# Layer 0 of a two-layer graph network in loops: the column that neighbouring windows share moves to TensorE, the kernels' products go by array halves behind the tiles

## The chip, the cores and the metric

The kernel runs on one NeuronCore of a Trainium2 chip. Five engines work side by side, each with an instruction queue of its own: TensorE (PE, its weight loads shown as PEld), VectorE (DVE), ScalarE (ACT), GpSimd (POOL) and SyncE (SP). They meet by semaphores alone. The metric is the device time of one execution in microseconds, lower is better. "Issue" in a profile is time in which an engine waited for nothing that the profile shows; "ACTq" is what ACT's queue itself runs, such as register instructions.

## The reference

There are 3125 nodes with 64 channels and 53125 edges, sorted by their target `dst`. Layer 0 is a spline convolution: an edge's three attributes give eight weights, its message is the sum over eight kernels of weight times `x[src] @ W[k]`, messages are averaged over the edges of a target, `x @ root` is added, then batch norm and ELU. Layer 1 sums `x[src] + edge_attr_64` over the edges of a target and applies a two-layer perceptron with batch norm. Each layer is added to its input and normalised.

```python
xj = x[src]
z = (B[:, :, None] * xj[:, None, :]).reshape(Etot, S * x.shape[1])
msg = z @ W.reshape(S * x.shape[1], W.shape[2])
agg = jax.ops.segment_sum(msg, dst, num_segments=x.shape[0])
cnt = jax.ops.segment_sum(jnp.ones((Etot,), dtype=x.dtype), dst, num_segments=x.shape[0])
out = agg / jnp.maximum(cnt, 1.0)[:, None] + x @ root
# layer 1
agg = jax.ops.segment_sum(node_feats[src] + edge_feats, dst, num_segments=n_nodes)
h = jax.nn.relu(agg @ W1 + b1) @ W2 + b2
```

## The kernel before

Edges are cut into T = 416 **tiles** of 128, one edge a partition, and eight tiles are a **chunk** (CH = 8, NCH = 52 chunks). As targets are sorted, a tile's targets lie in a **window** of WIN = 12 nodes from `base[g]` on. The next tile's window may begin with the target at which this one ends, so the two share a column.

*Per chunk.* POOL gathers `x[src]` for the chunk four ahead into `rows[:, s, t, 0:64]` with eight indirect DMAs (L296), once the z products of the slot's last chunk are done (`z_done`, L293). SP loads 256 KB of `edge_attr_64` into the other half of `rows` at the same moment (L249). Their loops are hardware loops over four chunks; PE, ACT and DVE have their 52 chunks written out.

DVE builds from comparisons with an iota, for the chunk ahead: `hot` (L730, position in the window), `whot` (L735, hot times eight weights and a one, fp32), `pair` (L746, source block and window position, bf16) and `ohp` (L752, source within its block, bf16).

*Per tile* (L404 to L417). PE runs `count_pairs(g + 1)` (L373), the counts of edges between 125 sources and 25 x 12 (block, window position) pairs, into one of MB = 3 banks of PSUM; the z product (L412), `rows` times `whot`, two fp32 passes; and `add_shared(g + 1)` (L380). For that, ACT's `keep_pairs(g)` copies the 25 counts of the column that the next window begins with into `shared` (L544), and PE adds them to the next tile's bank by an identity matrix.
*At the close of a chunk* PE counts edges (`count_edges`, L393, two fp32 passes over `ones`), sums the z of edge attributes (L385) and runs the eight 64 x 64 kernels (L388, two fp32 passes each) on `z_sb`, ACT's copy of z (L554, two halves), all into `t_ps`. DVE adds the eight windows of `t_ps` into `agg` two chunks later (L763), in order, each waiting for the one before. `whot` is built again only when `t_ready` says that the kernels are done (L733).

*After the loop* PE turns `agg` to node-major by 25 transposes of 65 partitions (L449, count included), DVE divides by the count, adds `xroot` and goes on with batch norm. Layer 1 multiplies a three-part bf16 table by `adj` (L473 over the whole array, L481 by halves of the array in turn).

Of the kernel before, what the change touches and what calls it, by code (L numbers as in the profile page):

```python
# [6 lines left out]
I32 = mybir.dt.int32  # L7
U8 = mybir.dt.uint8
F8 = mybir.dt.float8e4
BF16 = mybir.dt.bfloat16  # L10
# [5 lines left out]
def gnn_two_layers(nc, x, src, dst, ea3, ea64, wk_d, root_d, gamma0, beta0,  # L16
# [11 lines left out]
    AHEAD = SLOTS  # L28
    GATHERED = CH * 16
# [9 lines left out]
    NB = -(-NT // TPB)  # L39
    FULL = E // P  # L40
# [6 lines left out]
    MB = 3  # L47
# [14 lines left out]
    with ctx:  # L62
# [8 lines left out]
        idx = sb("idx", [P, SLOTS, CH], I32)  # L71
        dst_col = sb("dst_col", [P, T])
        rel = sb("rel", [P, T + CH])
        comb = sb("comb", [P, T + CH])
        srcp = sb("srcp", [P, T + CH])
# [4 lines left out]
        basis = sb("basis", [P, T + CH, KIN])  # L80
# [22 lines left out]
        z_sb = sb("z_sb", [P, CH, KIN, WIN])  # L103
# [21 lines left out]
        bank_sums = sb("bank_sums", [PN, 2, NB, C])  # L125
# [10 lines left out]
        shared = sb("shared", [PN, 2, NT], BF16)  # L136
        ident_h = sb("ident_h", [PN, PN], BF16)
# [21 lines left out]
        ident_h_ready = sem("ident_h_ready")  # L159
# [16 lines left out]
        hot_ready, whot_ready, oh_ready = sem("hot_ready"), sem("whot_ready"), sem("oh_ready")  # L176
        z_done, zsb_ready = sem("z_done"), sem("zsb_ready")
        t_ready, t_zeroed, added = sem("t_ready"), sem("t_zeroed"), sem("added")
        m_ready, shared_ready = sem("m_ready"), sem("shared_ready")
# [6 lines left out]
        turned0 = sem("turned0")  # L186
# [22 lines left out]

        def node_major(a):  # L210
            return a.rearrange("(t p) c -> p t c", p=PN)

# [67 lines left out]
        def _(pool):  # L280
# [5 lines left out]
            pool.wait_ge(ident_ready, 1)  # L286
            nc.gpsimd.tensor_copy(ident_h[:, :], ident[0:PN, 0:PN]).then_inc(ident_h_ready, 1)

            with pool.Fori(0, NCH // SLOTS) as i:
                for s in range(SLOTS):  # L290
                    c = i * SLOTS + s
                    pool.wait_ge(idx_ready, c + 1)
                    pool.wait_ge(z_done, c * 2 + 2)  # L293
                    pool.sem_inc(begun, 1)
                    for t in range(CH):
                        pool.indirect_dma_start(  # L296
                            rows[:, s, t, 0:C], None, x,
                            bass.IndirectOffsetOnAxis(ap=idx[:, s, t:t + 1], axis=0)).then_inc(gathered[s], 16)
# [22 lines left out]
        def _(pe):  # L321
# [46 lines left out]
            def count_pairs(g):  # L368
                c, t = g // CH, g % CH
                pe.wait_ge(oh_ready, c * 2 + t // (CH // 2) + 1)  # L370
                if g >= MB:
                    pe.wait_ge(adj_kept, g - MB + 1)
                last = nc.tensor.matmul(m_ps[0:PN, g % MB, 0:PAIRS], ohp[:, c % 2, t, :], pair[:, c % 2, t, :],  # L373
                                        start=True, stop=True)
                if g == 0:
                    last.then_inc(m_ready, 1)
# [616 lines left out]
```

## Time and profile before

| | us |
|---|---|
| median of 3 runs (range) | 989.84 (989.31 to 992.0) |
| profiled execution, its own time | 986.37 |
| its span | 984.6 |
| chunk loop of layer 0 | 45 to 831 |
| division, batch norm, layer norm, table | 831 to 886 |
| layer 1 | 886 to 985 |

Over the span PE is busy 69%, DVE 47%, ACT 34%, POOL 40%. The profiled execution is 1.8 us longer than its span, the part ahead of the first and behind the last instruction. Busy shares are means over stages with different limits, so the stages are read one by one.

### The profile page before, as it was taken

The numbers are of one execution on the slowest core, as the hardware profiler recorded it, in microseconds if no ns is written. First come the engines' busy times: TensorE is split into PE (matmuls) and PEld (weight loads), VectorE is DVE, ScalarE is ACT, GpSimd is POOL, SyncE is SP. The second block draws the span as 40 slices with busy tenths as digits, with TensorE's granted clock in tenths as the row PEclk, the third lists the DMA queues.
The fourth block names the chain that finished last, engine by engine and source line by source line (L and its number), as shares of the span: only waits on it lengthen the run. The fifth ranks groups of instructions, "written<-read, shape, count | busy, mean of one in ns | idle before, by whom it ended". The sixth has DMA issues, their size and how long they took to land.

```text
span 984.6 us, 15148 instructions
## 1 busy us (share of the span) xinstructions
PE 676.2 (69%) x3279; PEld 532.4 (54%) x3279; DVE 458.7 (47%) x953; ACT 330.3 (34%) x1040; POOL 397.5 (40%) x424
## 2 busy tenths in 40 slices
PE   3657686776867768677686776867768688309970
PEld 2546565655656556565565655656656576304540
DVE  8623434434444343443434434434344343599555
ACT  0224333343343433334334343343333434120120
POOL 4754544535445454454544635545445420000000
PEclk9655555555555555555555555555555557559985
DMA  4311111111112111111111211111111110000001
GB/s 96 73 29 37 30 39 28 41 36 32 38 28 42 36 32 38 28 41 38 31 39 28 42 36 32 39 28 42 37 30 40 26 21 2 0 0 1 1 1 33
DMA packets 76642, 31.26 MB, mean 32 GB/s; under 512 B 68528, under 2 KB 69901, under 8 KB 76557
## 3 DMA queue, kind: packets, MB, share of 16 engines
q1 hardware_dynamic: 63245, 16.67, 7.4%
q0 software_dynamic: 13312, 13.66, 7.4%
q8 instruction: 28, 0.46, 0.2%
q14 instruction: 57, 0.47, 0.2%
HBM read 29.50 MB, written 0.80 MB: 31 GB/s over the span
## 4 chain that ended last, share of the span: by engine, by line
PE 28%; issue 25%; ACTq 20%; ACT 16%; DVE 9%; another core or an unknown queue 1%; DVEq 0%
ACTq L544 9%; PE ps L388 8%; ACT adj L548 8%; ACTq L548 7%; ACT shared L544 5%; PE ps L412 5%; ACTq L540 4%; PE ps L473 4%; PE ps L373 3%; PE ps L380 2%; ACT z_sb L554 2%; PE ps L481 2%; PE ps L385 1%; PE ps L393 1%; DVE bank_sums L842 1%
## 5 line engine op out<-in xcount | busy, mean ns | idle before, releaser
L296 POOL DMA_INDIRECT rows<-in_x,idx x416 | 396.2, 952 | 398.5 <-PE ps L412 269.8
L380 PE MATMUL ps<-shared,ident_h 125*125 125x25 bf16 x415 | 121.8, 293 | 215.8 <-ACT shared L544 168.1
L412 PE MATMUL ps<-whot,rows 128*128 128x108 f32 x832 | 254.7, 408 | 0.0
L412 PEld LDWEIGHTS ps<-whot,rows 128*128 128x128 f32 x832 | 236.1, 329 | 11.3 <-issue 11.2
L548 ACT CAST adj<-ps 125x300 f32 x416 | 183.1, 440 | 142.3 <-issue 98.3
L380 PEld LDWEIGHTS ps<-shared,ident_h 125*125 125x125 bf16 x415 | 76.6, 185 | 276.0 <-ACT shared L544 187.7
L373 PE MATMUL ps<-pair,ohp 128*125 128x300 bf16 x416 | 201.5, 485 | 6.6 <-issue 6.6
L544 ACT CAST shared<-ps 125x25 bf16 x415 | 76.7, 185 | 341.9 <-issue 199.0
L763 DVE TENSOR_TENSOR agg<-agg,ps 128x24 f32 x416 | 74.5, 179 | 217.5 <-DVE agg L763 108.0
L735 DVE TENSOR_TENSOR whot<-ps,basis 128x864 f32<-128x864 f32 x52 | 55.0, 1058 | 253.2 <-PE ps L388 144.1
L746 DVE TENSOR_TENSOR pair<-ps,comb 128x1200 bf16<-128x1200 f32 x104 | 145.5, 1399 | 0.0
L388 PE MATMUL ps<-z_sb,wk 64*64 64x96 f32 x832 | 145.3, 365 | 0.0
L388 PEld LDWEIGHTS ps<-z_sb,wk 64*64 64x64 f32 x832 | 130.1, 222 | 11.5 <-issue 11.4
L373 PEld LDWEIGHTS ps<-pair,ohp 128*125 128x125 bf16 x416 | 89.3, 215 | 6.8 <-issue 6.8
L752 DVE TENSOR_TENSOR ohp<-ps,srcp 128x500 bf16<-128x500 f32 x104 | 69.6, 670 | 0.0
L554 ACT COPY z_sb<-ps 128x432 f32<-128x432 f32 x104 | 54.3, 522 | 8.7 <-remote 8.7
L473 PE MATMUL ps<-adj,basis 125*128 125x500 fp8e4 (+1 forms) x175 | 35.0, 363 | 22.1 <-DVE basis L931 22.1
L473 PEld LDWEIGHTS ps<-adj,basis 125*128 125x128 bf16 x175 | 16.4, 100 | 40.6 <-DVE basis L931 22.3
L385 PE MATMUL ps<-z_sb,ident 128*64 128x96 f32 x104 | 30.1, 392 | 1.3 <-ACT z_sb L554 1.1
L393 PE MATMUL ps<-whot,ones 128*64 128x96 f32 x104 | 30.1, 393 | 0.0
L936 DVE TENSOR_TENSOR pair<-pair,adj 125x785 int32<-125x785 int32 x23 | 22.5, 978 | 0.8
L624 ACT ACTIVATE u<-ps 64x500 f32<-64x500 f32 (+1 forms) x7 | 3.8, 538 | 54.8 <-PE ps L481 54.7
(135 smaller groups left out, 301.7 us busy)
## 6 DMA issues: line engine op xcount, KB each, us to landing
rows<-in_edge_attr SPq DMA_DIRECT2D x51, 256.0 KB
rows<-in_x,idx POOLq DMA_INDIRECT x416
x_nm<-in_x SPq DMA_DIRECT2D x1, 781.2 KB
out<-u SPq DMA_DIRECT2D x3, 218.8 KB
adj<-in_edge_attr SPq DMA_DIRECT2D x1, 576.0 KB
rows<-in_edge_attr SPq DMA_DIRECT2D x1, 224.0 KB
adj<-in_src SPq DMA_DIRECT2D x1, 192.0 KB
adj<-in_dst SPq DMA_DIRECT2D x1, 192.0 KB
```

Source lines behind the costliest of these rows:

```text
L296: pool.indirect_dma_start(rows[:, s, t, 0:C], None, x, bass.IndirectOffsetOnAxis(ap=idx[:, s, t:t + 1], axis=0)).then_inc(gathered[s], 16)
L373: last = nc.tensor.matmul(m_ps[0:PN, g % MB, 0:PAIRS], ohp[:, c % 2, t, :], pair[:, c % 2, t, :], start=True, stop=True)
L380: nc.tensor.matmul(m_ps[0:PN, g % MB, 0:PAIRS].rearrange("p (j w) -> p j w", w=WIN)[:, :, 0], ident_h[:, :], shared[:, (g - 1) % 2, :], st ...
L388: last = nc.tensor.matmul(t_ps[0:C, ts, 0:RW], wk[:, k, :], z_of[0:C, :, k, :], start=(k == 0), stop=(k == NK - 1))
L412: last = nc.tensor.matmul(z_ps[:, half, at:at + ZW], rows[:, s, t, :], whot[:, c % 2, t, :], start=True, stop=True)
L473: nc.tensor.matmul(ps[:, b, 0:min(AB, N - b * AB)], table[:, j, 0:P], adj_part(b, j), start=(j == 0), stop=False, skip_group_check=True)
L544: nc.scalar.copy(shared[:, g % 2, :], m_ps[0:PN, g % MB, bass.ds(turn, NT, WIN)]).then_inc(shared_ready, 1)
L548: nc.scalar.copy(adj[0:PN, :, bass.ds(start, WIN)], counts.rearrange("p (j w) -> p j w", w=WIN)).then_inc(adj_kept, 1)
L554: nc.scalar.copy(z_sb[:, half * n:(half + 1) * n, :, :], z_ps[:, half, 0:n * ZW].rearrange("p (w k n) -> p w k n", w=n, k=KIN)).then_inc(z ...
L746: nc.vector.tensor_tensor(pair[:, c % 2, half * n:(half + 1) * n, :], iota_to(PAIRS, n), each(comb[:, ts], PAIRS), ALU.is_equal)
L752: nc.vector.tensor_tensor(ohp[:, c % 2, half * n:(half + 1) * n, :], iota_to(PN, n), each(srcp[:, ts], PN), ALU.is_equal).then_inc(oh_read ...
L763: nc.vector.tensor_tensor(view, view, t_ps[:, c % 2, 0:2 * RW].rearrange("p (a w) -> p a w", a=2)[:, :, t * WIN:(t + 1) * WIN], ALU.add).t ...
```

## The change

It does five things in layer 0.

1. *The shared column.* ACT's copy into `shared`, the identity product `add_shared` and `ident_h` go. PE's `carry_over(c, t)` multiplies `ohp` of tile t once more, by the column of `pair` at position `turn` (the distance to the next window's start, a new row computed by DVE and loaded into a register by PE), and adds it to the bank of tile t + 1. `m_ready` counts these. There are MB = 2 banks, and `count_pairs` runs two tiles ahead, behind a wait for ACT's copy of the tile whose bank it takes.
2. *The kernels.* Even ones write partitions 0 to 63 and odd ones 64 to 127 of `t_ps`, by halves of the array, two partial sums. They run one chunk later: the ea sum and kernels 0, 1 behind tile 3 of the next chunk, 2, 3 behind tile 4, 4, 5 behind tile 5, 6, 7 behind tile 6. `z_sb` is double. The ea sum and the edge count change places, and the edge count is one bf16 pass over the upper halves of fp32 words.
4. *DVE's order.* The pairs of chunk c + 2, half of chunk c's starts, the sources (one instruction for eight tiles), the other starts, the weights, then the eight additions of chunk c, which wait for `t_ready` of the kernels that end in the next chunk. `whot` waits for `whot_used`, after the edge count.
5. *The division.* PE turns all 128 partitions in groups of four tiles and the counts by 25 transposes of one row; ACT copies the lower half of the channels' sums, DVE adds the upper, then divides and goes on as before. Layer 1's sums use the other halves of the partitions.

```diff
+    STEP = 2
+    IDXS = STEP * CH
-    MB = 3
+    MB = 2
...
-        z_sb = sb("z_sb", [P, CH, KIN, WIN])
+        z_sb = sb("z_sb", [P, 2, CH, KIN, WIN])
...
-            with pool.Fori(0, NCH // SLOTS) as i:
+            with nc.Fori(0, NCH // SLOTS, engines=[pool.engine], head_slot={pool.engine: 0}) as i:
...
+            def count_pairs(c, t, par=0):
+                if t == 0:
+                    pe.wait_ge(oh_ready, c + 1)
+                pe.wait_ge(adj_kept, c * CH + (t + 1))
+                return nc.tensor.matmul(m_ps[0:PN, t % MB, 0:PAIRS], ohp[:, par, t, :], pair[:, par, t, :],
                                         start=True, stop=True)
...
+            def carry_over(c, t, par):
+                at = pe.value_load(bass.AP(turn, offset=c * CH + t, ap=[[T, 1], [1, 1]]))
+                nc.tensor.matmul(
+                    m_ps[0:PN, (t + 1) % MB, 0:PAIRS].rearrange("p (j w) -> p j w", w=WIN)[:, :, 0],
+                    ohp[:, par, t, :],
+                    bass.AP(pair, offset=at + (par * CH + t) * PAIRS, ap=[[2 * CH * PAIRS, P], [WIN, NT]]),
+                    start=False, stop=True, skip_group_check=True).then_inc(m_ready, 1)
...
+            def through_kernels(par, z_of, ks):
+                for k in ks:
+                    low = C * (k % 2)
+                    last = nc.tensor.matmul(t_ps[low:low + C, par, 0:RW], wk[:, k, :], z_of[0:C, :, k, :],
+                                            start=(k < 2), stop=(k >= NK - 2))
+                return last
+
+            def count_edges(par, hot_of):
+                return nc.tensor.matmul(t_ps[0:C, par, RW:2 * RW], upper_halves(ones[:, 0:C]),
+                                        upper_halves(hot_of)[:, :, NK * WIN:ZW], start=True, stop=True)
...
+                for t in range(CH):
+                    carry_over(c, t, par)
+                    if t + 2 < CH:
+                        count_pairs(c, t + 2, par)
+                    else:
+                        count_pairs(i * SLOTS + (s + 1), t + 2 - CH, prev)
+                    half = t // (CH // 2)
+                    if t % (CH // 2) == 0:
+                        pe.wait_ge(zsb_ready, c * 2 + (half + 1))
                     at = (t % (CH // 2)) * ZW
+                    last = nc.tensor.matmul(z_ps[:, half, at:at + ZW], rows[:, s, t, :], whot[:, par, t, :],
                                             start=True, stop=True)
                     if t % (CH // 2) == CH // 2 - 1:
                         last.then_inc(z_done, 1)
+                    if first or t < CH // 2 - 1:
+                        continue
+                    if t == CH // 2 - 1:
+                        pe.wait_ge(zsb_ready, c * 2 + 2)
+                        sum_ea(prev, z_sb[:, prev, :, :, :])
+                        through_kernels(prev, z_sb[:, prev, :, :, :], (0, 1))
+                    elif t < CH - 2:
+                        n = 2 * (t - CH // 2 + 1)
+                        through_kernels(prev, z_sb[:, prev, :, :, :], (n, n + 1))
+                    elif t == CH - 2:
+                        through_kernels(prev, z_sb[:, prev, :, :, :], (NK - 2, NK - 1)).then_inc(t_ready, 1)
+                pe.wait_ge(added, c * CH + CH)
+                count_edges(par, whot[:, par, :, :]).then_inc(whot_used, 1)
+
+            for s in range(SLOTS):
+                chunk(0, s, first=(s == 0))
+            with pe.Fori(1, NCH // SLOTS) as i:
+                for s in range(SLOTS):
+                    chunk(i, s)
...
+            def keep_pairs(c, t):
+                start = act.value_load(bass.AP(base, offset=c * CH + t, ap=[[T, 1], [1, 1]]))
+                act.wait_ge(m_ready, c * CH + (t + 1))
+                act.wait_ge(adj_kept, c * CH + (t + MB))
+                nc.scalar.copy(bass.AP(adj, offset=start, ap=[[NT * NA, PN], [NA, NT], [1, WIN]]),
+                               m_ps[0:PN, t % MB, 0:PAIRS].rearrange("p (j w) -> p j w", w=WIN)
+                               ).then_inc(adj_kept, 1)
...
+            def two_chunks(i, first=False):
+                for par in range(STEP):
+                    c = i * STEP + par
+                    for t in range(CH):
+                        keep_pairs(c, t)
+                        if t == 0 and not (first and par == 0):
+                            keep_z(i * STEP + (par - 1), 1 - par, 1)
+                        elif t == CH // 2:
+                            keep_z(c, par, 0)
+                lay_out((i * STEP + AHEAD) * CH, (i & 1) * IDXS)
+
+            two_chunks(0, first=True)
+            with nc.Fori(1, NCH // STEP, engines=[act.engine], head_slot={act.engine: 0}) as i:
+                two_chunks(i)
...
+            for b in range(NQ):
+                ts = quad_tiles(b)
...
+                nc.scalar.copy(h[:, ts[0]:ts[-1] + 1, :], halves_of(b)[:, :, 0, :]).then_inc(half_kept, 1)
...
+            def add_windows(c, par, at):
+                dve.wait_ge(t_ready, c + 3)
+                for t in range(CH):
+                    view = bass.AP(agg, offset=at[t], ap=[[2 * NPAD, P], [NPAD, 2], [1, WIN]])
+                    dve.wait_ge(added, c * CH + (t + 2 * CH))
+                    nc.vector.tensor_tensor(
+                        view, view, t_ps[:, par, 0:2 * RW].rearrange("p (a w) -> p a w", a=2)[:, :, t * WIN:(t + 1) * WIN],
+                        ALU.add).then_inc(added, 1)
...
+            with nc.Fori(0, NCH // STEP, engines=[dve.engine], head_slot={dve.engine: 0}) as i:
+                for par in range(STEP):
+                    c, after = i * STEP + par, i * STEP + (par + STEP)
+                    dve.wait_ge(m_ready, c * CH + (CH + 1))
+                    for half in range(2):
+                        build_pairs(after, par, half)
+                    at = starts_of(c, range(CH // 2))
+                    build_sources(after, par)
+                    at += starts_of(c, range(CH // 2, CH))
+                    build_weights(after, par)
+                    add_windows(c, par, at)
...
+            def add_halves(b):
+                ts = quad_tiles(b)
+                dve.wait_ge(half_kept, b + 1)
+                nc.vector.tensor_tensor(h[:, ts[0]:ts[-1] + 1, :], h[:, ts[0]:ts[-1] + 1, :], halves_of(b)[:, :, 1, :],
+                                        ALU.add).then_inc(halves_added, 1)
```

## Rows read from the trace of the kernel before

**Rows 1.** The page: span, and the granted clock in 40 slices of 24.6 us.
```profile
span 984.6 us, 15148 instructions
...
PEclk9655555555555555555555555555555557559985
```
**Rows 2.** Busy time by stretch: stretch, us, then PE, PEld, DVE, ACT, POOL, PEclk, DMA, GB/s.
```profile
45.00:831.00 786.00, 569.63 (x2678) 465.81 (x2679) 326.18 (x712) 298.91 (x979) 370.69 (x393) 0.51 0.16 33
```
**Rows 3.** Waits from 45 to 831 us: us in total, times, longest.
```profile
POOL rows L296 <- PE ps L412: 269.8, 48, 8.6
ACT shared L544 <- issue: 199.0, 137, 4.3
...
PE ps L380 <- ACT shared L544: 168.1, 68, 6.7
```
**Rows 4.** Order of time, PE at a chunk's close: start, us, instruction.
```profile
510.53 0.58 PE L393 MATMUL ps<-whot,ones 128*64 128x96 f32 x2
...
511.49 2.82 PE L388 MATMUL ps<-z_sb,wk 64*64 64x96 f32 x16
...
514.23 0.76 PE L412 MATMUL ps<-whot,rows 128*128 128x108 f32 x2
```
**Rows 5.** Order of time, ACT in fast tiles.
```profile
524.42 0.41 ACT L548 CAST adj<-ps 125x300 f32 x1
...
525.31 0.41 ACT L548 CAST adj<-ps 125x300 f32 x1
```
**Rows 6.** Order of time, ACT across the slow stretch.
```profile
516.51 0.45 ACT L548 CAST adj<-ps 125x300 f32 x1
...
522.66 0.41 ACT L548 CAST adj<-ps 125x300 f32 x1
```
**Rows 7.** The chain of waits in that stretch: start, us, what.
```profile
517.22 0.70 ACTq L544
...
518.65 0.71 ACTq L544
```
**Rows 8.** Order of time, POOL: first and last gather of a chunk, next chunk's first.
```profile
510.91 0.94 POOL L296 DMA_INDIRECT rows<-in_x,idx  x1 [5.85 <-PE ps L412]
...
519.64 0.94 POOL L296 DMA_INDIRECT rows<-in_x,idx  x1 [0.30 <-issue]
526.15 0.94 POOL L296 DMA_INDIRECT rows<-in_x,idx  x1 [5.56 <-PE ps L412]
```
**Rows 9.** ACT's queue at L544: count, then least, median and longest ns.
```profile
L544 ACTq ALU_OP  x830: 2/38/709, 45.5 to 831.2; - x166
```
**Rows 10.** Groups by line, DVE, 45 to 831 us: count, busy us, mean ns.
```profile
L746 DVE TENSOR_TENSOR pair<-ps,comb 128x1200 bf16<-128x1200 f32 x103 | 144.1, 1399 | 0.0
...
L752 DVE TENSOR_TENSOR ohp<-ps,srcp 128x500 bf16<-128x500 f32 x103 | 69.0, 670 | 0.0
L735 DVE TENSOR_TENSOR whot<-ps,basis 128x864 f32<-128x864 f32 x51 | 53.9, 1058 | 253.2 <-PE ps L388 144.1 <-issue 109.1
```
**Rows 11.** Order of time, DVE: an addition and a one-hot.
```profile
508.88 0.18 DVE L763 TENSOR_TENSOR agg<-agg,ps 128x24 f32 x1 [0.47 <-DVE agg L763]
508.98 0.26 DVE L730 TENSOR_TENSOR ps<-ps,rel 128x96 f32<-128x96 f32 x1
```
**Rows 12.** Order of time, PE: tiles at the lower and the higher clock.
```profile
817.23 0.25 PE L380 MATMUL ps<-shared,ident_h 125*125 125x25 bf16 x1
...
817.98 0.30 PE L380 MATMUL ps<-shared,ident_h 125*125 125x25 bf16 x1
...
822.47 0.24 PE L380 MATMUL ps<-shared,ident_h 125*125 125x25 bf16 x1 [0.27 <-ACT shared L544]
...
823.35 0.24 PE L380 MATMUL ps<-shared,ident_h 125*125 125x25 bf16 x1 [0.27 <-ACT shared L544]
```
**Rows 13.** Busy time of L473, then of L481, in 10 us each: PE (count), PEld (count).
```profile
900.00:910.00 10.00, 10.00 (x55) 4.83 (x53) 1.00 0.00 0
...
922.00:932.00 10.00, 10.00 (x98) 5.28 (x94) 1.00 0.01 2
```

More of the change, by code:

```diff
@@ L39, in gnn_two_layers @@
     NB = -(-NT // TPB)
+    NQ = -(-NT // 4)
     FULL = E // P
@@ new lines, in count_edges, with chunk @@
+            def count_edges(par, hot_of):
+                return nc.tensor.matmul(t_ps[0:C, par, RW:2 * RW], upper_halves(ones[:, 0:C]),
+                                        upper_halves(hot_of)[:, :, NK * WIN:ZW], start=True, stop=True)
+            pe.wait_ge(t_ready, 2)
+            count_pairs(0, 0).then_inc(m_ready, 1)
+            count_pairs(0, 1)
+            def chunk(i, s, first=False):
+                c, par = i * SLOTS + s, s % 2
+                prev = 1 - par
+                pe.wait_ge(gathered[s], i * GATHERED + GATHERED)
+                pe.wait_ge(ea_loaded[s], i * 16 + 16)
@@ L411, in _ @@
                     at = (t % (CH // 2)) * ZW
-                    last = nc.tensor.matmul(z_ps[:, half, at:at + ZW], rows[:, s, t, :], whot[:, c % 2, t, :],
+                    last = nc.tensor.matmul(z_ps[:, half, at:at + ZW], rows[:, s, t, :], whot[:, par, t, :],
                                             start=True, stop=True)
@@ L739, in build_weights, with build_pairs @@
                     ALU.mult).then_inc(whot_ready, 1)
[L741 removed]
+            def build_pairs(c, par, half):
                 n = CH // 2
[L743 to L747 removed]
@@ L788, in _, with build_sources @@
-            dve.wait_ge(t_ready, NCH)
-            for t in range(CH):
-                g = (NCH - 1) * CH + t
-                add_window(start_of(g), g)
-            dve.wait_ge(added, T)
+                nc.vector.tensor_tensor(pair[:, par, half * n:(half + 1) * n, :], iota_to(PAIRS, n),
+                                        each(comb[:, bass.ds(c * CH + half * n, n)], PAIRS), ALU.is_equal)
+            def build_sources(c, par):
+                nc.vector.tensor_tensor(ohp[:, par, :, :], iota_to(PN, CH), each(srcp[:, bass.ds(c * CH, CH)], PN),
+                                        ALU.is_equal).then_inc(oh_ready, 1)
@@ new lines, in _ @@
+            nc.vector.memset(fb_hot[:, :], 0.0).then_inc(added, 2 * CH)
+            dve.wait_ge(xroot_ready, 1)
+            nc.vector.memset(adj[0:PN, :, N:NA], 0).then_inc(adj_kept, MB)
+            nc.vector.memset(fb_rel[:, :], 0.0).then_inc(zsb_ready, 2)
+            nc.vector.memset(over_row[:, :], 0.0).then_inc(whot_used, 1)
+            nc.vector.memset(t_ps, 0.0).then_inc(t_ready, 2)
+            for c in range(STEP):
+                for half in range(2):
+                    build_pairs(c, c, half)
+                build_sources(c, c)
+                build_weights(c, c)
```

247 lines of the change are left out of this document (86 added, 161 removed).

## Prediction

> **What bounds the kernel now.** I read the page first: 984.6 us, the TensorE clock in its lower level in nearly every slice [rows 1]. The execution took 986.4 us, 1.8 more than its span, and the median of the runs shown is 989.84, 3.5 more than that. Then the busy time by stage: layer 0's chunk loop runs from 45 to 831 us [rows 2]. It is 52 chunks of eight tiles, so 786 / 52 = 15.12 us a chunk, and 80% of the span. PE is busy 72% of that stage, DVE 41%, ACT 38%, POOL 47%: none is full. The waits of the stage say who holds whom: POOL waits for PE (z) 269.8 us, PE for ACT's copy of the shared column 168.1 us, and ACT for "issue", nothing that the profile shows, 199.0 us [rows 3].
>
> So I read one chunk in order of time. It has three parts. First, a **fast tile**: ACT's copies into adj come 0.89 us apart [rows 5]. Second, the **close** of a chunk: from the first edge-count pass at 510.53 to the next chunk's first z pass at 514.23, 3.70 us, in which PE takes no tile; the sixteen kernel passes take 2.74 of it, from 511.49 on [rows 4]. Third, a **slow stretch**: from the adj copy at 516.51 to the one two tiles on at 522.66 there are 6.15 us instead of 1.78, a loss of 4.4 [rows 6]. Eight tiles at 0.89, the close and the loss make 7.1 + 3.7 + 4.4 = 15.2. The three parts hold all of it.
>
> The chain of waits shows what the slow stretch is: ACT's queue spends 0.70 us on single register instructions (an ALU_OP of L544, a FUSED_REGOPS) [rows 7] whose median is 38 ns [rows 9]. Its place is tied to the gathers. Eight gathers start at 510.91 to 519.64, 1.25 us apart; the next eight wait until 526.15, 0.8 us after z is done [rows 8]. ACT is slow from 5.6 us after the first gather until 2.6 us after the last one's start. So a stretch of 11.3 us in each chunk is **under gathers**. By the code a tile costs ACT nine instructions, its two copies included: one load of the window's start, five register instructions that belong to turn, bound and address of two slices (L544 has 830 ALU_OP for 415 tiles [rows 9]), and one assertion. Under gathers it got through the last copy of a tile, two whole tiles at full speed, then about a dozen instructions in 5.7 us: some 31 in 11.3 us. Outside it does nine in 0.89 us. The account closes: 75 a chunk, 31 under gathers, 44 outside at 0.1 us make 4.4 + 11.3 = 15.7 us, against 15.1 measured. **ACT's instruction count, not its copying, sets the chunk.**
>
> **The change, part by part.**
> *Shared column on TensorE.* ACT loses one copy a tile and the subtraction, mask, address and assertion around it. What stays is load, register work for two loop-dependent waits and one address, and the copy: 4 to 7 instructions by the code, the trace of before having no such loop; I take 5. With two z copies, the index copy of every second chunk and the loop's own, 6 a chunk, that is 46 (38 to 62) instead of 75. PE's carry product has the same shape as add_shared's, so its time is the same. But PE now loads a register and forms an address for each tile; a load was not hidden for ACT in its 0.89. For PE I put 0.35 to 0.6 us of sequencer time, beside the 0.65 us in which the array works on the count and z products of the tile before; cover gone, it costs the 0.1 to 0.3 us that I keep in the tile below. The wait for adj_kept is new in depth (two banks for three): queued behind it on PE are z, the kernels and the next carry.
> *A tile on PE.* Undisturbed at the lower clock two tiles stand 0.75 us apart, and at the higher clock 0.88, where ACT set the pace [rows 12]. With the load I take 0.85 (0.75 to 0.95).
> *Kernels by halves, behind tiles.* Sixteen passes at 2.74 / 16 = 0.17 us. Layer 1 shows what halves do: passes of 500 columns over the whole array come 55 in 10 us, those that alternate halves 98 in 10 us [rows 13], so 1.8 at a time. Here two passes of one half follow each other, so half of that gain: 1.9 us (1.4 to 2.74). Edge count and ea sum share the 0.96 us ahead of the kernels [rows 4]; the edge count falls from two fp32 passes to one bf16, from 0.5 to 0.2, and the ea sum stays at 0.5. A chunk on PE alone is 8 x 0.85 + 1.9 + 0.2 + 0.5 = 9.4 us (7.8 to 11). What matters more: the close no longer parts ACT from its tiles.
> *DVE.* Pairs 2 x 1.40, sources 2 x 0.67, weights 1.06 [rows 10], one-hot 0.26, eight additions at 0.18 + 0.47 = 0.65 [rows 11] make 10.7 us. Dropping the assertions takes the additions to 0.5: 9.5 us. It lies beside PE and ACT, but its queue too is slow under gathers.
> *POOL.* Unchanged, 8 x 1.25 = 10.0 us a chunk [rows 8]: a floor.
> *Loops.* A back edge for every two chunks on ACT and DVE, every four on PE: 0 to 1 us each, mostly behind the wait for gathers; I take nothing and keep 0.2 a chunk for the range. The extra register step, the weights built after pairs and sources: first z product 1.6 us later (1.40 + 0.67 less what overlaps). The last eight additions, 8 x 0.15 = 1.2 us earlier. The division in halves: seven copies on ACT and seven additions on DVE, each 256 columns, nearest to the 0.41 us of ACT's 300 [rows 5]; most lies beside PE's transposes, and I put +1.1 us (0 to 4) where all of it was DVE's. Together +1.5.
>
> **The sum.** After z is done 0.8 us pass until the gathers, in which ACT does eight instructions; 31 more under gathers; 46 - 39 = 7 remain, 0.7 us. The chunk is 0.8 + 11.3 + 0.7 = 12.8 us. That leaves 15.12 - 12.8 = 2.32 us x 52 = 120.6 us. 986.4 - 120.6 + 1.5 = 867.3, and as a median 3.5 more: **871 us**. With 38 instructions nothing remains and the chunk is 12.1 (834 us); with 62 there remain 23 at 0.1, and it is 14.4 (954).
>
> **The clock.** The lower level is 1.2 GHz. In the slice of the page that holds 812 to 837 us the granted clock averages 0.7 [rows 1]: after tiles 0.75 to 0.89 us apart without a gap it rose to 2.4 GHz for a while, and a carry product took 0.24 us instead of 0.30, yet tiles still came 0.88 apart [rows 12]. PE will have fewer gaps. If it stays high, PE's 9.4 shrinks, which isn't what sets the chunk; it is worth nothing in the sum.
>
> **The rivals.**
> *A. The slow stretch goes.* If it comes from straight-line code and not from the gathers, a loop has none of it. Then POOL's 10.0 plus 0.3 sets the chunk: 986.4 - 52 x 4.82 + 5 = 741 us. For it: ACT and DVE are the engines with unrolled code. Against: its place moves with the gathers, not with the number of instructions. 0.13.
> *B. DVE's queue takes over.* It has 57 instructions a chunk now; by the code some 46 to 60 after. With 52, of which 31 under gathers and 5 ahead of them, 16 are left at its own pace of 7 a us, that of its additions: 12.1 + 2.3 = 14.4 us, 954 us. For it: DVE must finish pairs, additions and weights in turn, and its additions now wait for kernels that end in the next chunk's seventh tile. Against: it had slack of 4.5 us. 0.12.
> *C. The loops cost more than the code saves.* What ACT and DVE run at full speed at the start of the gathers, some 17 instructions, looks like a store filled while they idle. If a taken branch empties it, the next 17 come at 5.7 / 12 = 0.47 us instead of 0.1: 6.4 us for two chunks, 3.2 a chunk on the engine that branches under gathers, which DVE does. If it adds in full, the chunk is 16.0 and the time 1037 us; from 2.3 us a chunk on it is slower than before. Against: DVE's slack. 0.12.
> The Trainium skill ("Runtime: NRT & Kernel Launch", Instruction fetch mechanics) says that prefetch is purely sequential and that a branch out of the current window forces a fetch before execution goes on, so that unrolling is preferred. It would put this change on C's side; no row of this trace shows a branch on ACT, DVE or PE within the loop.
> *D. Nothing moves*: PE's register work under gathers is as slow as ACT's, and gains and losses meet. 0.03.
>
> **How the numbers follow.** Forecast (832 to 954 us) 0.60, A 0.13, B 0.12, C 0.12, D 0.03. A change under 0.3%, 3 us, can hardly be told from none. Faster: 0.60 + 0.13 + 0.12 = 0.85; same 0.03; slower 0.12. The range leaves out most of A and of C: 765 to 965.
>
> **What would show it.** Right: the stage lasts 52 x 12.8 = 666 us; ACT's shared copies are gone; its queue still has register steps of 0.7 us between 5 and 11 us after a chunk's first gather; PE's idle time is before count_pairs, released by ACT's adj copy; POOL waits some 2 us a chunk instead of 5.6. Wrong: gathers follow each other without a wait (A); PE waits for ohp or whot from DVE (B); gaps of several us at every second chunk (C); steps of 0.7 us in PE's own queue (D). The sum falls if ACT needs more than seven instructions a tile.

## Result and the profile after

The changed kernel takes 1098.35 us, the median of 4 runs (1081.65 to 1107.28), and the kernel before 989.58 beside it: 1.1008 times as long, interval 1.0866 to 1.115. The ratio is taken from its two executions in the faster of two states, 1097.67 and 1081.65 us. It is slower, where I had forecast 871 us.

The page of the changed kernel: span, and busy time of each engine with the count of instructions.

```profile
span 1095.9 us, 14862 instructions
...
PE 615.0 (56%) x3255; PEld 450.4 (41%) x3256; DVE 480.9 (44%) x916; ACT 269.7 (25%) x609; POOL 397.7 (36%) x423
...
PEclk9575555555555555555656555555555556557995
```

Busy time of the chunk loop, from the first adj copy to the last (stretch, us, then PE, PEld, DVE, ACT, POOL, PEclk, DMA, GB/s), answering to [rows 2]:

```profile
44.90:937.10 892.20, 503.27 (x2625) 379.15 (x2625) 339.17 (x661) 236.83 (x543) 371.00 (x394) 0.53 0.13 29
```

892.2 / 52 = 17.16 us a chunk. By the same rule the kernel before has 46.1 to 832.8, 15.13 a chunk, so the loop lost 105.5 us. What lies around it grew from 197.9 to 203.7. No engine has a larger share of the loop than before (DVE 38% against 41%, POOL 42% against 47%): PE worked 503 us of it and stood idle for the rest. The waits of the whole span say where (us in total, times, longest), answering to [rows 3]:

```profile
POOL rows L311 <- ACT idx L559: 340.9, 22, 16.8
...
ACT adj L581 <- remote: 329.2, 41, 13.0
PE ps L387 <- ACT adj L581: 264.2, 30, 15.9
...
DVE agg L806 <- remote: 66.9, 4, 16.7
ACT z_sb L590 <- remote: 56.3, 17, 4.4
```

There are two new things. POOL now waits for the indices, once in two chunks, some 16 us, and hardly for z (43.0 us in all). And ACT waits 385.5 us for "remote": a semaphore step that reached it at a moment when nothing recorded on this core had just ended. DVE has 66.9 us of it too, where the kernel before has none. ACT had 24.4 us of it there, in two lines:

```profile
ACT shared L544 <- remote: 15.7, 12, 2.7
ACT z_sb L554 <- remote: 8.7, 10, 1.9
```

One such wait in order of time, in the changed kernel. POOL first (start, us, instruction; in brackets the idle time before it):

```profile
498.19 0.94 POOL L311 DMA_INDIRECT rows<-in_x,idx  x1 [12.56 <-ACT idx L559]
...
516.92 0.94 POOL L311 DMA_INDIRECT rows<-in_x,idx  x1 [0.31 <-issue]
532.99 0.94 POOL L311 DMA_INDIRECT rows<-in_x,idx  x1 [15.12 <-PE ps L433]
```

From the first of these rows to the second there are sixteen gathers, both counted, 1.25 us apart without a pause, where [rows 8] had eight and a pause of 5.6 us. Then ACT:

```profile
503.99 0.45 ACT L581 CAST adj<-ps 125x300 f32 x1 [2.53 <-PE ps L392]
508.14 0.52 ACT L590 COPY z_sb<-ps 128x432 f32<-128x432 f32 x1 [3.70 <-remote]
520.90 1.01 ACT L581 CAST adj<-ps 125x300 f32 x2 [12.24 <-remote]
```

And PE:

```profile
503.38 0.30 PE L392 MATMUL ps<-pair,ohp 128*125 x1
504.50 0.51 PE L387 MATMUL ps<-pair,ohp 128*125 128x300 bf16 x1 [0.82 <-issue]
...
505.85 0.30 PE L392 MATMUL ps<-pair,ohp 128*125 x1
521.41 0.51 PE L387 MATMUL ps<-pair,ohp 128*125 128x300 bf16 x1 [15.26 <-ACT adj L581]
```

The first adj copy at 520.90 needs the carry product that began at 503.38 and ended at 503.68: ACT saw the step 17 us late. It saw the next one (505.85) with it; the "x2" is two copies back to back. In the other direction nothing is late: PE's count product at 504.50 starts 0.06 us after ACT's copy of 503.99 ends, and over the whole trace none starts more than 0.4 us after both the copy that it waits for and PE's last product. ACT is free again 3.8 us after the start of the sixteenth gather. I call this a **late step**, and the gathers that start 1.25 us apart a **row**.

### The profile page after: what moved, and what is told of

Its sections match the earlier page's. It is cut to its first block, busy times and chain, and to the rows that moved or that the text cites. A ratio compares the mean times of both kernels' runs of the same rounds, so it can differ in the third digit from the quotient of the medians.

```text
span 1095.9 us, 14862 instructions
## 1 busy us (share of the span) xinstructions
PE 615.0 (56%) x3255; PEld 450.4 (41%) x3256; DVE 480.9 (44%) x916; ACT 269.7 (25%) x609; POOL 397.7 (36%) x423
## 4 chain that ended last, share of the span: by engine, by line
PE 45%; another core or an unknown queue 36%; DVE 8%; issue 6%; ACT 2%; ACTq 2%; DVEq 1%
PE ps L433 12%; PE ps L387 11%; PE ps L405 7%; PE ps L392 5%; PE ps L513 3%; PE ps L399 2%; PE ps L521 2%; ACT adj L581 1%; ACTq L578 1%; DVE z_sb L882 1%; PE ps L410 1%; PE ps L377 1%; DVEq L799 1%; PE ps L545 1%
## 5 line engine op out<-in xcount | busy, mean ns | idle before, releaser
L581 ACT CAST adj<-ps 125x300 f32 x416 | 183.2, 440 | 581.1 <-remote 329.2
L387 PEld LDWEIGHTS ps<-pair,ohp 128*125 128x125 bf16 x418 | 82.4, 197 | 412.2 <-ACT adj L581 260.5
L433 PE MATMUL ps<-whot,rows 128*128 128x108 f32 x832 | 239.4, 388 | 0.0
L433 PEld LDWEIGHTS ps<-whot,rows 128*128 128x128 f32 x832 | 232.0, 321 | 0.0
L392 PE MATMUL ps<-pair,ohp 128*125 x416 | 114.9, 276 | 3.3 <-issue 2.7
L405 PE MATMUL ps<-z_sb,wk 64*64 64x96 f32 x832 | 114.9, 373 | 0.0
L392 PEld LDWEIGHTS ps<-pair,ohp 128*125 128x125 bf16 x416 | 75.7, 182 | 52.8 <-issue 44.3
L405 PEld LDWEIGHTS ps<-z_sb,wk 64*64 64x64 f32 x832 | 58.0, 193 | 37.9 <-issue 34.5
L795 DVE TENSOR_TENSOR ohp<-ps,srcp 128x1000 bf16<-128x1000 f32 x54 | 64.3, 1190 | 0.0
L778 DVE TENSOR_TENSOR ps<-ps,rel 128x96 f32<-128x96 f32 x54 | 14.4, 266 | 46.2 <-issue 46.1
L399 PEld LDWEIGHTS ps<-z_sb,ident 128*64 128x64 f32 x104 | 14.1, 193 | 9.9 <-issue 8.8
L521 PE MATMUL ps<-adj,basis 125*64 125x500 fp8e4 (+1 forms) x175 | 17.3, 353 | 0.0
```

The source lines that it names most:

```text
L387: return nc.tensor.matmul(m_ps[0:PN, t % MB, 0:PAIRS], ohp[:, par, t, :], pair[:, par, t, :], start=True, stop=True)
L392: nc.tensor.matmul(m_ps[0:PN, (t + 1) % MB, 0:PAIRS].rearrange("p (j w) -> p j w", w=WIN)[:, :, 0], ohp[:, par, t, :], bass.AP(pair, offse ...
L399: nc.tensor.matmul(t_ps[C:P, par, RW:2 * RW], ident[:, C:P], z_of[:, :, NK, :], start=True, stop=True)
L405: last = nc.tensor.matmul(t_ps[low:low + C, par, 0:RW], wk[:, k, :], z_of[0:C, :, k, :], start=(k < 2), stop=(k >= NK - 2))
L433: last = nc.tensor.matmul(z_ps[:, half, at:at + ZW], rows[:, s, t, :], whot[:, par, t, :], start=True, stop=True)
L581: nc.scalar.copy(bass.AP(adj, offset=start, ap=[[NT * NA, PN], [NA, NT], [1, WIN]]), m_ps[0:PN, t % MB, 0:PAIRS].rearrange("p (j w) -> p j ...
```

## Experiments

Ratios are to the kernel before on the same chip in the same session, with intervals.

### The loops, and the length of a row

**Written out.** `with nc.Fori(...) as i:` becomes `for i in range(...):` in PE, ACT, DVE and POOL.

> The changed kernel with the loops of layer 0 on TensorE, VectorE, ScalarE and GpSimd written out chunk by chunk, so that every wait is against a constant and no branch is left; the indices are still laid out for two chunks at once. SyncE's loop stays. Theory (gathers): in the profile of the changed kernel GpSimd gathers 16 times in a row (498.2 to 516.9 us), and from about 5 us after the first to 3.8 us after the last the semaphore and register steps of the other engines crawl; that hangs on the row of gathers, so this kernel keeps it: 1060 to 1110 us, one gap of 10 us or more on ScalarE in each two chunks. Rival (loops): the gaps are waits against a register or the jump back, so written out they go and the time falls to 870 or less.

1.0333 (1.0309 to 1.0358): above what the rival allows, a little below the theory's range. ACT still waits 305.7 us for remote at L581, so the late steps need neither a wait against a register nor a branch. The changed kernel itself wasn't measured beside it. Nearest to it on this chip is the one without TensorE's load, further below, with its loops: 1092.69 us, 45 us above these 1047.89. As that load costs nothing in the kernel before, some 4% seem to be the loops' in rows of 16; by what, no run shows.

**Indices per chunk.**

```diff
-                lay_out((i * STEP + AHEAD) * CH, (i & 1) * IDXS)
+                    lay_out((c + AHEAD) * CH, (i & 1) * IDXS + par * CH, CH)
```

> The changed kernel, loops kept, but ScalarE lays the indices out for one chunk at a time (8 columns behind each chunk's last tile) and GpSimd waits for them at each chunk, so a row of gathers is 8 long and not 16. Theory (gathers): the crawl of about 17 us in each two chunks (from 5 us after the first of 16 gathers to 3.8 us after the last) becomes two of about 6 to 8 us, so two chunks take 35.6 - 2 to 5 us: 970 to 1050 us; with a pause of GpSimd of a few us in each chunk. Rival (loops): nothing changes, 1085 to 1110 us.

0.9964 (0.9942 to 0.9987), 1011.61 us. Halving the row takes away the slowdown: 17.16 us a chunk (on this chip 17.00 without TensorE's load, (930.2 - 46.1) / 52) become (852.0 - 47.7) / 52 = 15.47. But the late steps don't go, they come in each chunk, 357.0 us of remote in all. PE's carry product, and then ACT's copies around it:

```profile
401.99 0.30 PE L391 MATMUL ps<-pair,ohp 128*125 x1
```

```profile
401.07 0.52 ACT L589 COPY z_sb<-ps 128x432 f32<-128x432 f32 x1 [0.24 <-PE ps L432]
409.85 1.00 ACT L580 CAST adj<-ps 125x300 f32 x2 [8.26 <-remote]
```

The carry product ends 4.1 us behind the row's first gather, at 398.18, and is seen 7.4 us later, 2.8 after the start of its last, at 406.93.

**One gather, and four, of each chunk's eight** (`for t in range(1)` and `range(4)` in POOL's loop, the rows filled once with a constant).

> The changed kernel with only the first of each chunk's eight gathers issued (rows of tiles 1 to 7 hold a constant in their source half), 52 gathers instead of 416; all else as it is. Theory (gathers): no gap of more than 2 us is left on ScalarE; a chunk takes what the undisturbed stretches show, 8 tiles of 0.75 to 0.87 us and 2 to 3 us of kernels: 9 to 10 us, so 655 to 720 us in all. Rival (loops): the gaps stay, 1050 us or more.

> The changed kernel with the first four of each chunk's eight gathers issued (rows of tiles 4 to 7 hold a constant in their source half): 8 gathers in a row in each two chunks instead of 16. Theory (gathers): the crawl starts 5 us after the first gather and ends 2.6 to 3.8 us after the start of the last (8.75 us behind the first), so it is 6.5 to 7.5 us in two chunks instead of 17: two chunks take 24 to 27 us, 790 to 880 us in all. If instead gaps come in proportion to the number of gathers, 850 to 900. Rival (loops): 1050 us or more.

691.73 and 847.26 us, one execution each, and each within its theory's range. The second lies 3 us from the 850 to 900 of gaps in proportion to the gathers, so it doesn't part these two. With one gather no wait for remote is left, and a chunk takes (531.3 - 44.6) / 52 = 9.36 us. SP's loads of 256 KB a chunk are all still there (51 of them), so they don't make the late steps alone. With four (a row of eight in two chunks) there are 138.2 us of it.

**The same, done to the kernel before.** Its two `lay_out` calls for a pair of chunks come behind the odd chunk's last tile:

```diff
-                if c + AHEAD < NCH:
-                    lay_out(c + AHEAD, c % SLOTS)
...
+                for d in (c - 1, c):
+                    if c % 2 == 1 and d + AHEAD < NCH:
+                        lay_out(d + AHEAD, d % SLOTS)
```

> The kernel before with one thing of the change: the indices of two chunks are laid out one behind the other, after each odd chunk's last tile, in place of one chunk's in the middle of each chunk. So GpSimd gathers in rows of 16 as in the changed kernel, while ScalarE still copies the shared column and all is written out. Theory (row of gathers): rows of 16 alone lengthen it, since the stretch of ScalarE's 0.7 us register steps is 16.3 us of two chunks instead of 2 x 5.7: about 5 us more for each two chunks, and the pause of GpSimd between rows adds its own wait: 1.08 to 1.18 times the kernel before. Rival (the harm is in TensorE's waits for ScalarE, which are only in the changed kernel): 0.99 to 1.03 times.

1.136 (1.1339 to 1.1381). This one edit, alone, costs more than the whole change did (1.1008, in another session). It also hands the indices over later, and POOL waits 425.9 us for them; in the changed kernel the same order costs nothing once the gathers are spaced (0.8422 below). Its chain of waits shows the price in a row of 16 that began at 452.21 (start, us, what):

```profile
467.18 0.70 ACTq L548
467.88 0.71 issue
468.59 0.69 ACTq L548
469.28 0.71 issue
469.99 0.69 ACTq L540
```

In a row of eight the register steps followed each other every 0.7 us: right behind the second of [rows 7], at 518.65, comes

```profile
519.38 0.70 ACTq L548
```

In the row of 16, behind the twelfth gather each is followed by as long a gap, and they are 1.4 us apart.

### Is it what TensorE loads?

After the first runs I held PE's new register load for the cause: PE had never been slow before, and now it reads a register from memory in each tile. One kernel takes the load away (`at = 0`), one adds it to the kernel before (`pe.value_load(base[0:1, g:g + 1])` in `add_shared`).

> The changed kernel without TensorE's register load of `turn` in carry_over: the shared column is always column 0 (a constant address), so the counts are others; every matmul and every copy stays. After the first four runs: in a row of gathers TensorE's steps of m_ready reach ScalarE late, together, some 3 us after the start of the last gather (written out as well as in loops). Theory (TensorE's loads): an engine that reads registers from memory while the gathers run is slowed, and TensorE, which was free of it before, now is; without its loads m_ready is seen within 1 us and the time falls from 1.10 times the kernel before to 0.80 to 0.95 times. Rival (gathers alone): m_ready stays late whatever TensorE loads, 1.07 to 1.11 times.

> The kernel before with one register load from `base` added on TensorE in each tile, ahead of the wait for the shared column; the value is not used. Theory (TensorE's loads): the added load makes TensorE's steps late under gathers, so the slow stretch of each chunk grows: 1.03 to 1.15 times the kernel before. Rival (gathers alone): the load costs 0.3 us in TensorE's instruction queue, beside its waits: 0.99 to 1.02 times.

1.0764 (1.0704 to 1.0824) and 0.9988 (0.9967 to 1.0008). ACT's wait for remote at L581 is 339.5 us without the load. The theory fell.

### Breaking the row

**A wait for the landing** after every fourth, and after every second gather, on the kernel with indices per chunk:

```diff
+                        if t % 4 == 3:
+                            pool.wait_ge(gathered[s], i * GATHERED + (t + 1) * 16)
+                            pool.sem_inc(begun, 1)
```

> The kernel of the second run (indices laid out per chunk) with GpSimd waiting after every fourth gather until it has landed. Four gathers start over 3.75 us and the last lands some 2.1 us after its start, so a chunk's gathers take 2 x 6.2 = 12.4 us. Theory (length of the row): m_ready came late only for steps more than 3 us behind the first gather of a row, so with rows of four the late steps wait 1 to 3 us instead of 6: a chunk 12.4 to 14 us, 0.85 to 0.94 times the kernel before. Rival (each gather costs the same, however spaced): no gain, 0.99 to 1.03 times, or worse by the added waits.

> As the kernel with waits after every fourth gather, but after every second. Gathers: 4 x (1.25 + 2.1 + 0.3) = 14.6 us a chunk. Theory (length of the row): no step is late at all, TensorE waits only for rows: a chunk 14 to 15 us, 0.93 to 1.0 times the kernel before, and no gap of over 2 us on ScalarE within a chunk. Rival (each gather costs the same): gaps of 2 us or more remain and the chunk is 16 us or more.

0.9435 (0.9418 to 0.9452) and 1.1384 (1.135 to 1.1419). ACT's waits for remote fall from 357 us to 3.8 and to none, and the first lands at the upper edge of its theory's range. Not all is on time in rows of four: 49 adj copies still start over 1 us after both their carry product and ACT's last instruction ended, but 2.5 us at most, where rows of eight had 66 and up to 7.8. The time of the second isn't what I expected: POOL's own chain is 18.2 us a chunk ((993.1 - 44.5) / 52), not 14.6. I had left out what it takes from a landing to the next start.

**The same pause in the kernel before, and written out.**

> The kernel before with GpSimd waiting after every fourth gather until it has landed, and nothing else. In the changed kernel with indices per chunk that pause gave 0.9435 against 0.9964. Theory (row of gathers): here ScalarE's slow steps (about 4.4 us a chunk lost) go, but GpSimd's own 2 x 7 us a chunk becomes the bound with its slack: a chunk 14 to 14.6 us, 0.93 to 0.97 times. Rival (the pause helps only where TensorE's step must wake ScalarE): 0.99 to 1.04 times.

> The kernel with indices per chunk and a wait after every fourth gather, its loops on TensorE, ScalarE, VectorE and GpSimd written out. Written out, the changed kernel went from 1.10 to 1.033. Theory (GpSimd is the bound there: 14.4 us a chunk, of which 0.8 us twice is its own steps between landing and the next gather): only these steps get cheaper, 0.92 to 0.945 times the kernel before. Rival (loop registers slow TensorE and ScalarE): 0.87 to 0.91 times.

0.9202 (0.9186 to 0.9217), better than I expected, and 0.9172 (0.9152 to 0.9191), a little under the theory's range and above the rival's. The pause helps the kernel before as well, by 8%, with no other change. POOL is the bound in both.

**Two in flight.** Odd gathers get a semaphore of their own, and a gather starts when the one before the last has landed:

```diff
+                        of = (gathered, gathered_odd)[t % 2][s]
+                        if t >= 2:
+                            pool.wait_ge(of, i * GATHERED + t // 2 * 16)
+                            pool.sem_inc(begun, 1)
```

> The kernel with indices per chunk, and GpSimd starts a gather only when the one before the last has landed (two semaphores in turn): no pause in a chunk's eight, but 1.45 us from start to start instead of 1.25. Theory (rate: something fills up because gathers start every 1.25 us): at 1.45 us it fills later or not at all, m_ready is late by less than 3 us, 0.90 to 0.96 times the kernel before. Rival (it takes a pause in which nothing is in flight): m_ready is as late as before it, now in a row of 10.2 us instead of 8.75: 0.99 to 1.08 times.

0.8398 (0.8383 to 0.8412), 853.48 us, the best of all on these chips and below the range I gave. POOL in order of time:

```profile
411.19 0.94 POOL L315 DMA_INDIRECT rows<-in_x,idx  x1 [0.99 <-issue]
412.44 0.94 POOL L315 DMA_INDIRECT rows<-in_x,idx  x1 [0.31 <-issue]
414.39 0.94 POOL L315 DMA_INDIRECT rows<-in_x,idx  x1 [1.01 <-issue]
```

Gathers now go mostly in pairs, 1.25 and 1.95 us apart. The first two of a chunk wait for no landing, so where a chunk begins up to four follow each other at 1.25 us. The longest pause from 46 to 530 us is 2.5 us, the mean distance is 1.6 us instead of 1.25, and ACT's waits for remote are 4.9 + 5.3 us; 28 adj copies are still over 1 us late, by 2.5 at most. So a pause in which all has landed isn't needed. A chunk takes (692.9 - 46.0) / 52 = 12.44 us.

> The kernel before, in which GpSimd starts a gather only when the one before the last has landed (two semaphores in turn), and nothing else. In the changed kernel with indices per chunk this gave 0.8398. Theory (the rest of the change gains once the lateness is gone): here ScalarE's and TensorE's close of 3.7 us and 8 tiles of 0.89 us stay, 10.8 us a chunk at best, but GpSimd needs 4 x (1.25 + 1.94) = 12.8 us: 0.84 to 0.88 times the kernel before, so within 0.04 of the changed kernel. Rival (the rest of the change is worth its 2.3 us a chunk whatever GpSimd does): 0.93 to 0.97 times.

> The kernel with indices per chunk and two gathers in flight (0.8398), its loops on TensorE, ScalarE, VectorE and GpSimd written out. Theory (GpSimd's gathers are the bound there, with 0.2 us of register steps in each of four waits): 0.80 to 0.84 times the kernel before. Rival (the loops cost nothing there): 0.835 to 0.845 times, the same.

> The changed kernel as it is (indices of two chunks at once, rows of 16 gathers) with two gathers in flight at most. Theory (spacing keeps the engines free however long the row is): no step of m_ready is late by more than 3 us; but a row of 16 now takes 25.5 us, and the indices of the next come only behind the second chunk's last tile, so GpSimd pauses more than with indices per chunk: 0.86 to 0.93 times the kernel before. Rival (the length of the row counts even when spaced): 1.0 to 1.1 times.

> The kernel with indices per chunk, with GpSimd filling a tile of its own (128x256) after every gather and waiting for that fill before its next step: gathers start further apart (an estimate from the 204 ns that its 128x128 fill takes: 1.5 to 1.7 us), with no wait for a landing anywhere. Theory (distance): the lateness goes as with two in flight: 0.84 to 0.90 times the kernel before. Rival (it takes a wait for a landing, so that few are in flight): m_ready still comes late in each chunk, 0.98 to 1.05 times.

0.8489 (0.8441 to 0.8536), 0.8457 (0.8438 to 0.8476), 0.8422 (0.8382 to 0.8461) and 0.9275 (0.9239 to 0.931). Four answers. With two in flight the kernel before is as fast to about 1%, as the theory had it: POOL's gathers hide all that the change saves. Written out is no faster, against the theory, so the loops cost nothing there. The indices of two chunks at once do no harm when the row is spaced (15.3 us of remote), so that run came out below its theory's range. And distance alone, 1.44 us by a fill and no wait for a landing, leaves 146.4 us of remote at L586 and lands between theory and rival: late steps again, but shorter (4.1 us the longest). Whether two in flight does better for its 1.6 us or for its waits, these two don't part.

### A chip without late steps

The last two kernels ran on a third chip.

> The kernel before with only the first of each chunk's eight gathers issued (rows of tiles 1 to 7 hold a constant in their source half). The changed kernel with one gather a chunk took 691.7 us. Theory (my sum's terms: 8 tiles of 0.89 us and a close of 3.70 us are 10.8 us a chunk, outside of any gathers; the start and the end as they are): 989.8 - 52 x 4.3 = 766 us, 740 to 790, so the rest of the change is worth 50 to 100 us when no gathers disturb it. Rival (the rest of the change brings nothing by itself): 680 to 705 us.

> The changed kernel with the indices laid out per chunk (0.9964), its loops on TensorE, ScalarE, VectorE and GpSimd written out. Theory (fewer register steps on ScalarE and VectorE meet the slow stretch, so more tiles get through it): as with rows of 16, where writing out took 6 per cent, a smaller gain here: 0.94 to 0.98 times the kernel before. Rival (the loops cost nothing of their own; what was gained there came from where the gathers fell): 0.985 to 1.005 times.

There the kernel before took 766.16 us (753.38 to 775.56, 7 runs), against 989.58 in the comparison above and 1012 to 1016 on the two chips of the other experiments. Its time goes with the mean granted clock (753.38 us at 0.652, 775.56 at 0.576), so I compare at like clocks. With one gather a chunk it took 766.6 us at 0.603, and with all gathers 766.16 at 0.602: on this chip the gathers cost it nothing. That the 770.2 (the median) fell into my range is in part luck, since I had meant a chip where the gathers cost it 4.3 us a chunk. The changed kernel with indices per chunk, written out, took 705.37 at 0.64, against 754.5, the mean of the two runs of the kernel before at 0.64 and 0.65: 0.935 of it; what the loops cost under late steps, which I had meant it to show, it could not tell here. Its waits of POOL and its instructions at L580, ACT's copy and its register step (count, then least, median and longest ns):

```profile
POOL rows L310 <- issue: 124.3, 408, 0.3
...
L580 ACT CAST adj<-ps x389: 408/449/458, 59.8 to 529.3; 125x300 f32 x195
L580 ACTq ALU_OP  x388: 35/35/35, 60.5 to 529.2; - x194
```

POOL gathers 1.25 us apart from 31.9 to 533.7 us, one row of some 400, and nothing is late: no wait for remote, a chunk of (545.4 - 45.0) / 52 = 9.62 us. So the late steps aren't bound up with gathers as such. The chips differ, by what, no run here shows. No trace was taken of the kernel before on this one. The changed kernel itself, and those that space the gathers, weren't run there. As kernels with two in flight take 12.4 us a chunk for POOL's sake, I'd expect them to lose on it; that is argued, not shown.

## Why the prediction was wrong

**The step that failed is POOL's**: "Unchanged, 8 x 1.25 = 10.0 us a chunk [rows 8]: a floor". The time of a gather is unchanged. When they start is not. I counted "the index copy of every second chunk" as one more instruction of ACT, and did not ask who waits for it: by the code it stands behind the second chunk's last tile, POOL waits for it, and then has two chunks' slots free at once. Eight and eight become sixteen. The sum then used "a stretch of 11.3 us in each chunk", read from rows of eight. So rows of 16 never entered the sum. The kernel before with that one edit shows their price: (997.7 - 45.6) / 52 = 18.31 us a chunk instead of 15.13.

**Seeing the row would not have saved the sum**, and that is the second failed step, the sentence in bold: "ACT's instruction count, not its copying, sets the chunk". By that account two chunks with one row of 16 take 0.8 us, then 18.75 + 2.6 under gathers with 17 + 33 of the 92 instructions, then the last 34 at 0.1: 25.6 us, 12.8 a chunk as before. Measured are 17.16. The account closed for the kernel before to 0.6 us, and was a description of it, not the cause. I read the slow stretch as a rate of ACT's queue, 0.7 us an instruction, and took the rate along. In the changed kernel ACT's register steps at L580 never take over 35 ns, its loads never over 313:

```profile
L580 ACTq ALU_OP  x400: 35/35/35, 70.2 to 937.0; - x134
...
L578 ACTq TENSOR_LOAD <-base x387: 272/278/313, 59.9 to 897.3; - x194
...
L799 DVEq TENSOR_LOAD <-base x370: 4/301/715, 63.0 to 879.8; - x185
```

DVE's loads do still reach 0.7 us (the third row). ACT has few instructions left, comes early to its wait for PE and then hears of PE's step only when the row is over. So the count of its instructions no longer buys time. With rows of eight, on one chip, a chunk takes 15.47 us in the changed kernel and 15.56 in the kernel before with the harmless load ((858.1 - 48.9) / 52). With rows of 16 it takes 17.16 and 18.31, in two sessions. With rows of like length the changed kernel is no slower, and next to nothing faster in rows of eight: its rows of 16 made it slower, and what I had saved on ACT was not worth the 2.3 us of my sum. That the row is the cause on these chips is shown, by one gather, rows of eight, rows of four, and rows of 16 in the kernel before. Why the same row shows as slow register steps in one kernel and as late steps in the other is not, nor is the split fixed: the kernel before with the load waits 141.2 us for remote (83.6 + 57.6), against 24.4 without it, in the trace of before.

**Terms that held.** A chunk on PE alone, 9.4 us: 9.36 with one gather, but the match is luck. At the lower clock, 0.50 from 299.9 to 310 us, eight tiles of that kernel take 9.99 us from carry product to carry product:

```profile
299.99 0.25 PE L393 MATMUL ps<-pair,ohp 128*125 x1
...
302.03 0.30 PE L393 MATMUL ps<-pair,ohp 128*125 x1
...
303.49 0.30 PE L393 MATMUL ps<-pair,ohp 128*125 x1
...
309.98 0.25 PE L393 MATMUL ps<-pair,ohp 128*125 x1
```

A tile with two kernels takes 1.46 us (second and third row) and one without 0.74 to 0.88, so the eight kernels cost some 2.6 us where the sum had 1.9. In a few chunks the granted clock rose to 1.0, and there eight tiles took 7.6 us; that makes the mean. Neither bounded the changed kernel. The three parts of the kernel before without the slow stretch, 7.1 + 3.7 = 10.8: (612.6 - 43.9) / 52 = 10.94. So the change is worth (770.2 - 691.7) / 52 = 1.5 us a chunk where nothing is late; both kernels had one gather a chunk, on two chips and at unlike clocks (0.60 and 0.63). On the third chip at like clocks, all gathers in and written out, it is (754.5 - 705.4) / 52 = 0.9. B did not come: PE waits for ohp 0.4 us in the loop. D did not come: PE's register loads (L391) take 494 ns at most.

```profile
L391 PEldq TENSOR_LOAD <-turn x416: 294/301/494, 45.5 to 936.3; - x139
...
L606 ACTq COMPARE_BRANCH  x26: 38/45/54, 69.3 to 937.5; - x26
```

**Terms that were off.** Around the loop I put +1.5 us; it was +5.8. It is all behind the loop, 158.8 us instead of 151.8, where I had 0 to 4 for the division; ahead of it 1.2 us were gained. The kernels took 2.6 us for 1.9, as above.

**Rival C** came nearest, for another reason. It gave 1037 us, a chance of 0.12, and foresaw gaps at every second chunk, and gaps there are. But ACT's jump back takes 45 ns (the row above) and its queue goes on 0.11 us later, written out 305.7 us of late steps stay, and with two in flight writing out gains nothing. Only the 4% in rows of 16 speak for a share of the loops. The Trainium skill ("Runtime: NRT & Kernel Launch", Instruction fetch mechanics) prefers unrolling, as a taken branch out of the window waits for a fetch; no row here shows such a wait at these loops. **Rival A** was right that the slow stretch can go, as the third chip shows, and wrong on the reason: there the written-out kernel before gains nothing from fewer gathers, so by its times, not by a trace, the stretch is gone from it as well.

**The range** of 765 to 965 held neither 1098 nor a case like it, since all my cases but C kept the gathers' rhythm. "POOL waits some 2 us a chunk" was the sign to look at: it waited 15.1 us for two.

## What to carry to other kernels

When a change moves the step that a queue waits for, write down that queue's new order of starts before any sum; a handshake issued half as often makes bursts twice as long. Where a profile shows slow register steps or waits for "remote" beside a row of gathers, space the gathers (here two in flight, a few lines of code) before tuning what is slowed: that gave 15% to the untouched kernel, where the change alone lost 10%. And measure on more than one chip, as a cost of over 200 us on one may be none on the next.

## What the runs showed of the hardware

- In the first comparison, and on two of the three chips of the experiments, indirect gathers that start 1.25 us apart delay other engines from some 4 us behind the first on: register steps of ACT and DVE take 0.7 us each in a row of eight, 1.4 us from step to step late in a row of 16, and steps from PE to ACT come up to 17 us late (503.68 to 520.90). All is over 2.6 to 3.8 us after the last start. Steps from ACT to PE are not late (0.06 us at 504.50, never over 0.4), nor are PE's register loads slow (494 ns at most).
- With rows of four, or with two in flight, little is late: 3.8 and 10 us of ACT's remote waits, against 357, and adj copies late by 2.5 us at most, against 7.8.
- On a third chip none of this happened, with 400 gathers in a row in the one kernel traced there with all its gathers.
